# Placing the second chunk of the first batch otherwise, and carrying the stacks in fewer transfers

## What is computed

```python
x = x + 0.5 * ffn(layernorm(x), router_w, router_b, expert_weights)   # 8 experts of 128x128, top 2
x = x + attn(layernorm(x), wq, wk_down, wv_down, wk_up, wv_up, wo)
x = x + 0.5 * ffn(layernorm(x), router_w, router_b, expert_weights)
# attn: D_LAT = 32, N_HEADS, N_KV = 8, 2
q = (x @ wq).reshape(B, T, 2, 4, 128)
k_lat, v_lat = (x @ wk_down).reshape(B, T, 2, 32), (x @ wv_down).reshape(B, T, 2, 32)
k, v = k_lat @ wk_up, v_lat @ wv_up
probs = softmax(where(causal, q @ k.T * 128 ** -0.5, min))
return (probs @ v).reshape(B, T, 1024) @ wo
```

## Time and profile before

| | us |
|---|---|
| median of three runs | 678.4 |
| lowest, highest | 676.56, 681.41 |
| the profiled execution, time | 677.78 |
| its span | 676.0 |
| PE busy | 553.4 (82%) |
| DVE busy | 406.7 (60%) |
| ACT busy | 355.1 (53%) |
| POOL busy | 153.3 (23%) |

### The profile page before, as it was taken

One profiled execution on the slowest core, in us unless ns is written; L12 is line 12 of the kernel. 1 busy time (PEld: TensorE's weight loads), 2 busy tenths in 40 slices (PEclk: granted clock), 3 DMA queues, 4 the chain that ended last, 5 costly groups with the idle time before them and its releaser, 6 DMA issues.

```text
span 676.0 us, 10472 instructions
## 1 busy us (share of the span) xinstructions
PE 553.4 (82%) x3342; PEld 240.0 (36%) x3342; DVE 406.7 (60%) x1500; ACT 355.1 (53%) x841; POOL 153.3 (23%) x257
## 2 busy tenths in 40 slices
PE   3825687898989889989889779988899789899836
PEld 2512234243432343334424433334334332333332
DVE  4343576777665675865667475865756756473225
ACT  2232254367555744757657444748556554476612
POOL 2130410034100102531004302511025110143213
PEclk9957779699999997999999979999999987999958
DMA  4002001000111000001101000001101000000000
GB/s 130 0 16 58 18 24 36 2 12 6 40 46 27 25 2 0 17 19 45 43 8 29 13 16 2 1 12 46 36 3 41 16 3 0 1 17 16 17 0 16
DMA packets 23816, 14.56 MB, mean 22 GB/s; under 512 B 5640, under 2 KB 23632, under 8 KB 23760
## 3 DMA queue, kind: packets, MB, share of 16 engines
q1 hardware_dynamic: 23184, 13.49, 7.3%
q10 hardware_dynamic: 576, 0.39, 0.2%
HBM read 3.78 MB, written 2.10 MB: 9 GB/s over the span
## 4 chain that ended last, share of the span: by engine, by line
PE 55%; DVE 17%; ACT 10%; issue 7%; POOL 4%; SPq 4%; ACTq 1%; DMA 1%; POOLq 0%; DVEq 0%
PE bank L1088 13%; PE bank L1157 10%; PE bank L1160 8%; PE bank L1138 7%; PE bank L1125 6%; SPq L505 3%; DVE masked L899 3%; ACT scaled L657 3%; ACT prob L699 3%; DVE m_part L902 2%; PE bank L1080 2%; ACT xn L632 2%; DVE dve_sum L872 2%; PE bank L1171 2%; DVE bank L824 2%
## 5 line engine op out<-in xcount | busy, mean ns | idle before, releaser
L699 ACT ACTIVATE prob<-bank,exp_scale 128x512 f32<-128x512 f32 (+3 forms) x384 | 214.3, 583 | 202.3 <-PE bank L1141 146.5
L899 DVE CUSTOM_DVE_ANT_0 masked<-bank,mask_qk 128x128 f32<-128x128 f32 (+3 forms) x256 | 122.4, 485 | 111.2 <-PE bank L1125 110.0
L1125 PE MATMUL bank<-k_stack,q_stack 96*128 96x512 f16 (+3 forms) x384 | 132.2, 349 | 37.3 <-DVE m_part L902 11.0
L1088 PE MATMUL bank<-we,xT 128*128 128x512 f32 x256 | 143.8, 657 | 20.6 <-ACT scaled L657 15.7
L1138 PE MATMUL bank<-q_stack,k_stack 98*128 98x512 f16 (+3 forms) x384 | 128.7, 342 | 7.3 <-ACT prob L699 5.4
L902 DVE TENSOR_REDUCE m_part<-bank 128x1 f32<-128x512 f32 x128 | 87.4, 683 | 38.5 <-PE bank L1125 38.0
L573 POOL TENSOR_TENSOR pair_sum<-dve_sum,scaled 128x256 f32<-128x256 f32 x64 | 46.6, 728 | 255.4 <-DVE dve_sum L872 215.9
L1157 PE MATMUL bank<-prob,v_lat 128*32 128x512 f32 (+3 forms) x768 | 86.6, 524 | 0.5 <-ACT prob L699 0.5
L657 ACT ACTIVATE scaled<-bank,gate 128x128 f32<-128x128 f32 x256 | 72.7, 373 | 24.6 <-PE bank L1088 11.4
L1160 PE MATMUL bank<-prob,ones 128*32 128x512 f32 (+3 forms) x768 | 84.0, 510 | 0.0
L1138 PEld LDWEIGHTS bank<-q_stack,k_stack 98*128 98x128 f16 x384 | 39.4, 103 | 92.7 <-issue 48.2
(11 more groups left out here) (106 smaller groups left out, 502.9 us busy)
## 6 DMA issues: line engine op xcount, KB each, us to landing
q_stack<-q_hi SPq DMA_DIRECT2D x120, 32.0 KB, 1.8
x<-in_L_attn_x SPq DMA_DIRECT2D x8, 256.0 KB, 2.8
out_x<-x SPq DMA_DIRECT2D x8, 256.0 KB, 2.3
q_stack<-q_lo SPq DMA_DIRECT2D x60, 32.0 KB, 1.9
k_stack<-k_hi SPq DMA_DIRECT2D x32, 32.0 KB, 1.8
we<-in_L_ffn_expert_weights SPq DMA_DIRECT2D x1, 512.0 KB, 4.2
x<-in_L_attn_wq SPq DMA_DIRECT2D x1, 512.0 KB, 6.0
x<-in_L_attn_wo SPq DMA_DIRECT2D x1, 512.0 KB, 7.2
```

The lines of the kernel that those rows point to most:

```text
L699: nc.scalar.activation(into, bank[ST + n % NST][:, 0:w], ACT.Exp, scale=exp_scale[:, 0:1]).then_inc(p_ready, 1)
L899: V.tensor_tensor_reduce(out=masked[:, m % 2, 0:w], in0=seen, in1=mask_qk[:, CH - w:CH], op0=ALU.add, op1=ALU.max, scale=1.0, scalar=LOWES ...
L1088: mm(take_fb(("y", f, n, j))[:], x_part(2 * f, n, t * P, (t + 1) * P), we[:, cols(half)], start=True, stop=True).then_inc(y_done, 1)
L1125: mm(into[:, 0:w], q_stack[0:MROW, c, g * NR + r, (i % TC) * P:(i % TC + 1) * P], k_stack[0:MROW, b % 2, g, k:k + w], start=True, stop=Tru ...
```

## The change

Chunk 1 of batch 0 gets a pace of its own, SECOND, and starts at slot -64. Its first norm, its transposes (-57) and its router matmuls (-56) so stand ahead of chunk 0's expert tiles, its routing stands behind chunk 0's second statistics (-39 to -35), and its expert tiles at -27 to -18. The maxima of quad 0 move to -18 to -3, the row to -1, and those of quads 1 and 2 follow from -2 at three every five slots.

The queries of a group are kept with the heads interleaved in the partitions (partition 4 l + r instead of 32 r + l), the keys with the groups interleaved (2 l + g). For that ACT writes aq in two permuted copies and makes a permuted copy down_k of the key weights. One transfer then carries four heads (128 KB) or both groups of keys (64 KB): 3 for keys and 6 for queries a chunk, all on SP. Keys get semaphores of their own, k_stacked; PE waits for those of every chunk up to its own as well as for stacked, and ACT waits before q_hi for the stack of the batch before.

```diff
+SECOND = Pace(bn=0, stats=1, stat_slots=2, power=3, xn=4, xt=7, xt_step=0, logits=8, route=25, route_slots=5, y=37,
+              bn_1=4, stats_1=14, power_1=16, xn_1=17, xt_1=20, key=22, query=23, query_step=1, value=26)
-FRONT = [Unit(0, 0, 0, 1, -70, QUICK), Unit(0, 1, 1, 1, -46, QUICK)] \
+FRONT = [Unit(0, 0, 0, 1, -70, QUICK), Unit(0, 1, 1, 1, -64, SECOND)] \
...
-def stack_slot(n, g, r, planned):
+def stack_slot(n, g, planned):
...
-    free = (b - 1) * NS + QSTART[q] + NR * QTILES[q] + 2 + 3 * r
+    free = (b - 1) * NS + QSTART[q] + NR * QTILES[q] + 2
...
-            _k = _y + _p.key + 2 + 6 * _g
-            PLAN["stack_keys", _k].append((_n, _g))
-            for _r in range(NR):
-                PLAN["stack_queries", stack_slot(_n, _g, _r, _k + 1 + _r)].append((_n, _g, _r))
+            _k = _y + _p.key + 2 + (_p.query_step + 1) * _g
+            if _g == 0:
+                PLAN["stack_keys", _k].append(_n)
+            PLAN["stack_queries", stack_slot(_n, _g, _k + 1)].append((_n, _g))
...
-        return -22 + ls if q == 0 else -6 + (ls - QSTART[1]) * 2 // 3
+        return -18 + ls if q == 0 else -2 + (ls - QSTART[1]) * 3 // 5
...
-        STACK_DMAS = 3 * (NR + 1)
+        STACK_DMAS = 3
...
-            def stack_keys(n, g):
+            def stack_keys(n):
...
                 for i, part in enumerate((k_hi, k_hi, k_lo)):
-                    sp.dma_start(k_stack[i * DL:(i + 1) * DL, b % 2, g, cols(c)],
-                                 part[rows, n % 2, :]).then_inc(stacked[c * NKV + g], N_DMA)
+                    sp.dma_start(k_stack[i * DL:(i + 1) * DL, b % 2, :, cols(c)],
+                                 part[:, n % 2, :]).then_inc(k_stacked[c], N_DMA)
-            def stack_queries(n, g, r):
+            def stack_queries(n, g):
...
                 for i, part in enumerate((q_hi, q_lo, q_hi)):
-                    sp.dma_start(q_stack[i * DL:(i + 1) * DL, c, g * NR + r, :],
-                                 part[rows, n % 2, g, :]).then_inc(stacked[q], N_DMA)
+                    sp.dma_start(q_stack[i * DL:(i + 1) * DL, c, g * NR:(g + 1) * NR, :],
+                                 part[:, n % 2, g, :]).then_inc(stacked[q], N_DMA)
...
+                copy(down_k[:].rearrange("p (l g) -> p l g", g=NKV),
+                     down[:, 0:NKV * DL].rearrange("p (g l) -> p l g", g=NKV)).then_inc(prep_act, 1)
...
-                copy(aq[:], bank[OB][:, 0:NH * DL]).then_inc(prep_act, 1)
+                for g in range(NKV):
+                    copy(aq[:, g * P:(g + 1) * P].rearrange("p (l r) -> p l r", r=NR),
+                         bank[OB][:, g * P:(g + 1) * P].rearrange("p (r l) -> p l r", r=NR)).then_inc(prep_act, 1)
...
             def keys(n):
                 b, c = divmod(n, NC)
-                for g in range(NKV):
-                    need(act, stacked[c * NKV + g], b * STACK_DMAS * N_DMA)
+                need(act, k_stacked[c], b * STACK_DMAS * N_DMA)
...
             def queries(n, g):
+                b, c = divmod(n, NC)
+                need(act, stacked[c * NKV + g], b * STACK_DMAS * N_DMA)
                 act.wait_ge(q_done, n * NKV + g + 1)
...
-            def stack_queries(g):
-
-                act.wait_ge(qlo_ready, g + 1)
-                for r in range(NR // 2, NR):
-                    rows = slice(r * DL, (r + 1) * DL)
-                    for i, part in enumerate((q_hi, q_lo, q_hi)):
-                        act.dma_start(q_stack[i * DL:(i + 1) * DL, 0, g * NR + r, :],
-                                      part[rows, 0, g, :]).then_inc(stacked[g], N_DMA)
...
-                mm(into[0:nk, :], down[:, 0:nk], x_part(1, n), start=True, stop=True).then_inc(k_done, 1)
+                mm(into[0:nk, :], down_k[:], x_part(1, n), start=True, stop=True).then_inc(k_done, 1)
...
                 if m == quad_maxima(b * NQ + q) - NR * QTILES[q]:
+                    for k_c in range(c + 1):
+                        pe.wait_ge(k_stacked[k_c], (b + 1) * STACK_DMAS * N_DMA)
                     pe.wait_ge(stacked[q], (b + 1) * STACK_DMAS * N_DMA)
```

More of the change, by code:

```diff
@@ L306, in macaron @@
         down = sb("down", [P, 2 * NKV * DL])
+        down_k = sb("down_k", [P, NKV * DL])
         we = sb("we", [P, NE * D])
@@ L401, in macaron @@
         v_ready = sem("v_ready")
+        k_stacked = sems("k_stacked", NC)
         stacked = sems("stacked", NQ)
@@ L492, in stack_keys @@
                 need(sp, st_done, (b - 1) * NS)
-                rows = slice(g * DL, (g + 1) * DL)
                 for i, part in enumerate((k_hi, k_hi, k_lo)):
-                    sp.dma_start(k_stack[i * DL:(i + 1) * DL, b % 2, g, cols(c)],
-                                 part[rows, n % 2, :]).then_inc(stacked[c * NKV + g], N_DMA)
-            def stack_queries(n, g, r):
+                    sp.dma_start(k_stack[i * DL:(i + 1) * DL, b % 2, :, cols(c)],
+                                 part[:, n % 2, :]).then_inc(k_stacked[c], N_DMA)
+            def stack_queries(n, g):
                 b, c = divmod(n, NC)
@@ L517, in _ @@
                     stack_maxima(ROW_AT[s])
-                for n, g in PLAN["stack_keys", s]:
-                    stack_keys(n, g)
-                for n, g, r in PLAN["stack_queries", s]:
-                    if n or r < NR // 2:
-                        stack_queries(n, g, r)
+                for n in PLAN["stack_keys", s]:
+                    stack_keys(n)
+                for n, g in PLAN["stack_queries", s]:
+                    stack_queries(n, g)
                 for n in PLAN["load", s]:
@@ L727, in _ @@
                     queries(n, g)
-                    if n == 0:
-                        stack_queries(g)
                 for n in PLAN["value_copy", s]:
@@ L1001, in prepare_rest @@
                     last.then_inc(prep_pe, 1)
-                pe.wait_ge(prep_act, 4)
+                pe.wait_ge(prep_act, 5)
                 for h in range(NH):
```

4 lines of the change are left out of this document (2 added, 2 removed).

## The result

| | before | after |
|---|---|---|
| median of 20 runs each, us | 676.64 | 669.37 |
| lowest, highest | 672.61, 681.52 | 667.84, 676.2 |
| the profiled execution, time | 677.78 | 671.65 |
| its span | 676.0 | 669.9 |
| mean granted clock | 0.918 | 0.926 |

The changed kernel takes 0.9905 of the time of the kernel before, with a 95% interval of 0.9881 to 0.9928. So the gain is clear of noise both times, but small: 7.3 us of the median here and 3.8 there. 670.0 us was forecast and 669.37 measured.

The account below looks back on a forecast made before the run. TensorE was taken to bound the steady part, a chain of latencies the front up to the first score. Terms -7.5 + 2.5 - 3.4 = -8.4 us took 677.8 to 669.4, median 670.0; range 662 to 679.

Parts of the forecast that it names:

- (a): Chunk 1's first norm, transposes and router ahead of chunk 0's tiles: experts +2.3 us, last step -1.9, chunk 0 ends 0.4 later.
- (b): Chunk 0's second norm to its stacks: key 0.9 us earlier, k_lo 1.4 earlier, queries' matmuls end at 56.1.
- rival 4: Front: chunk 1's x lands only near 12 us, making all some 2.5 later, 672.5; chance 0.02.
- (c): Chunk 0's stack transfers, 30 before, 9 on SyncE after: issue 0.6 us, landing at most 2.8, hidden before the first maxima.
- (d): Chunk 1's expert tiles: without issues on ScalarE, scaling starts at 58.1 to 59.0, tiles 7.0 us earlier (6.1 to 7.9).
- (e): Chunk 1's last tile to the first score: old order and 17.5 us, less 0.5 on DVE; first score at 90.0.
- (f): Slots 0 to 26: five more blocks of maxima behind the first score cost 2.5 us, at most 3.4.
- rival 1: Behind the first score the gain is given back: -3.6, 674.8; sign: slot 16's score beyond 26 us behind it; chance 0.27.
- (g): PE waits on stacks, mostly later batches: 60 transfers a batch become 18, -3.4 us (between 0 and 4.7).
- rival 2: Front: clock comes back sooner, chunk 1's key and query records run at 0.47 us, 3 less, 667; chance 0.16.
- rival 3: 97.5 to 676 us: denser PE work lowers the granted clock; 0.018 eats the gain, 0.04 gives 688; chance 0.06.

Follow-up runs that it names:

- Experiment 3: Kernel before with only ScalarE's 12 query transfers of chunk 0 issued by SyncE, still 32 KB each: 669.95 us, ratio 0.9894.
- experiments 1 to 3: Kernel before with the change's placement alone (1.0015); kernel after with the old placement (0.9909); kernel before with ScalarE's 12 issues moved to SyncE (0.9894).
- Experiment 5: Kernel after with chunk 1's stack transfers planned three slots later, so SyncE issues the row of maxima first: 670.32 us, ratio 0.9919.
- experiment 7: Kernel after with each 128 KB query transfer split by columns into two of 64 KB: 670.96 us in one execution.
- experiment 10: Kernel after run again unchanged, on one chip with a run of the early maxima: 673.29 us, ratio 0.9948 to the kernel before.
- experiment 2: Kernel after with the old unit of chunk 1 and old places of the maxima, leaving the large transfers alone: 670.91 us, ratio 0.9909.
- the early maxima: Kernel after with only the maxima back at their old places (quad 0 from slot -22, others from -6), run twice: 667.54 and 667.63 us.
- experiment 6: Kernel after with the maxima two slots earlier (quad 0 from -20, the others from -4, three every two slots): 671.01 us, ratio 0.9929.

## Why the prediction was right, and where it was not

**(a), (b)** held within half a microsecond: experts at 26.94 (27.1), the last tile of chunk 0 ends at 43.77 (near 43.5), k_lo 1.2 earlier (1.4), q_hi of group 1 at 56.18 (56.1). Chunk 1's early norm cost nothing, so rival 4 is false: its x was there at 9.69 us, not near 12, and its norm ran in ScalarE's idle time at 13.4 us.

**(c)** Issue is 0.60 us at 128 KB, as taken. Landing is 3.2 to 3.3, above the "at most" of 2.8 that I took from the 256 KB load. A load from memory was not a bound for a transfer from one part of SBUF to 32 partitions of another. It was hidden all the same for the queries, with less room than forecast: the first maximum, due after 66 us, ran at 62.02 and waited for no DMA. It mattered one step further on.

The rule of the Trainium skill that I weighed ("DMA: Bandwidth & Descriptors", "Issuing engines are not separate DMA queues", issue time "usually small relative to the DMA itself") would, by my estimate in the prediction, have had the 12 issues worth under 1 us. Experiment 3, which moves them and does nothing else, gained 1.06% (0.71 to 1.41), 7.2 us. The row decides, as the sum had it: 0.61 us of queue against 1.9 to landing is a third, and the queue was that of an engine with work in the chain.

**(d)** Scaling at 58.01 (58.1 to 59.0), GpSimd at 60.16 (60.3 to 62.1), last tile 8.0 earlier where 7.0 was taken: just beyond the near end of the range (6.1 to 7.9). The term left open how fast the tiles' records would run; they took 0.45 us each (12 in 5.37 from 56.81), against 0.92 before (six in 5.49 from 67.70). The mechanism is shown by experiments 1 to 3. What the prediction left open was whose merit it is; scaling begins at 66.20 with the placement alone and at 58.45 with the issues alone, so it is the issues'.

**(e)** was off in a term. From the last tile to the first score the kernel before took 17.5 us, after 18.5 (72.03 to 90.51), forecast 17.0. Tile to key is 7.84 in both. Key to mT_lo is 6.95 against 7.15, so of the 0.5 expected on DVE 0.2 came. From the row's first issue to the score it is 3.37 against 2.40: this is the 1.0. The step that failed is the one that put the row's two transfers "behind six others on SyncE as before" and so took no change. Six others are six issues still, but behind large ones the row landed 2.7 us after its second issue instead of 1.8. Experiment 5, with the row ahead of them, and experiment 7, with halves, have the 1.8 again.

**(f)** had the right sign and too small a price. 2.5 was taken and 3.4 was the upper end. Cut in four, the kernel after against the kernel before gives -1.0, +2.3, +0.6 and +1.5: net 3.4, gross 4.4; in experiment 10 7.2 net. The -1.0 is about the stack wait of 0.9 that the kernel before had there, but experiment 2 has no such wait either and took 11.5 us, so that isn't settled. The step that failed is the size of a block: "at most 5 x 0.69" counts one engine's time for it, and DVE's is even less, 2.2 us for all five. Against the early maxima at nearly the same clock, slots 8 to 16 and 24 to 32 show 1.9 + 1.5 = 3.4 for the four blocks more in them. That this equals the upper end is chance, and a fall of the granted clock in slots 8 to 16, 0 to 3.7 us from one execution to another, was in no term. This is rival 1's place and mechanism at part of its price: its test, slot 16's score beyond 26 us, was not met in the profile of the kernel after (24.0 us from exponent to exponent) and was met in experiment 10 (27.8).

**(g)** was too large, with 3.4. PE waits for no query stack any more, as forecast. But of the waits of the earlier trace rows only two are seen again as steps in the time of the slots: 0.9 us near slot 4 and 1.45 at 188 us, in slots 32 to 64, which took 47.4 us instead of 48.9. The later ones (0.44 and 0.99 us) don't show beside the differences of the clock, and with experiment 2 at 47.5 and experiment 3 at 48.4 us for slots 32 to 64 the ratios of these two still don't differ. I put it at 2.5, the 1.0 of slots 0 to 8 with it.

**The sum**, term by term from the starts of the exponents: the front -6.8 (forecast -7.5), slots 0 to 32 +4.4 gross (+2.5), waits -2.5 (-3.4), and -1.1 in later stretches, where the granted clocks differ and which no term had: -6.0. Three errors of one sign, 3.5 together, and 1.1 that came back unforecast.

That 670.0 met 669.37 so closely is luck in part. The forecast started from 678.4, the median of three runs, where 20 gave 676.64; this 1.8 too much hid that the gain was 7.3 and not 8.4. In the second comparison the gain was 3.8 us and the median 673.29, which lies in the range that the prediction gave to rival 1 (673 to 679). What came out as reasoned is where the gain comes from, ScalarE's issues; the price behind the first score was taken too low.

**Rivals 2 and 3.** Chunk 1's key still ran at 0.97 us a record (two in 1.94 at 79.42), and 60 to 80 us has a clock of 0.74 as before: no sign of rival 2 where it was looked for, though the tiles before that key did run faster (above, (d)). The steady part has 0.99 and not 0.95: no sign of rival 3, in either profile of the kernel after.

## What to carry to other kernels

An engine whose work stands in the chain should issue no DMAs; here each took 0.6 us of its queue, whatever its size, and the sign of it was "issue" as what ended its idle time. Where a chain ends in a transfer, send it early and leave ready work to stand beside it: with the early maxima the first score was no later, and behind it the same blocks cost more (3.4 us) than their own time on DVE (2.2). Judge a reordering not by when the bound stretch starts but by when a fixed later piece of work does: here the exponent of slot 32, which told more than the first score but misled for experiment 6. And measure the parts of a placement one by one: here one gained what the other lost.
